# Two decoder layers on one core: the output product of the first cross attention in three fp32r terms, with its operands split by GpSimd

## What is computed

```
q = rmsnorm((x_norm @ Wq + bq) as 16 heads of 128) * qn_w
k = rmsnorm((ctx @ Wk + bk) as 4 heads of 128) * kn_w
v = (ctx @ Wv + bv) as 4 heads of 128           # each serves 4 query heads
probs = softmax(q @ k.T / sqrt(128) + mask)      # 256 x 64 for each head
x = x + tanh(gate) * (concat(probs @ v) @ Wo)
```

## Time and profile before

| what | value |
|---|---|
| median of 3 runs | 1886.22 us (1883.31 to 1887.39) |
| the profiled execution | 1881.76 us, span 1880.0 us |
| mean granted TensorE clock | 0.974 |
| TensorE matmul / weight load busy | 1743.0 us (93%) / 1570.9 us (84%) |
| VectorE, ScalarE, GpSimd busy | 1095.1 (58%), 1318.6 (70%), 1065.5 us (57%) |
| output products of the stage (L765) | 256 passes, from 111.5 to 367.8 us |

### The profile page before, as it was taken

The page is one execution under the profiler, slowest core; times in us unless marked ns, Lnnn a source line. Parts: engine busy times, 40 slices in busy tenths (PEclk is TensorE's granted clock), DMA queues, the critical chain, the costliest instruction groups (busy, mean ns, idle before and its releaser), DMA issues.

```text
span 1880.0 us, 36601 instructions
## 1 busy us (share of the span) xinstructions
PE 1743.0 (93%) x11648; PEld 1570.9 (84%) x11648; DVE 1095.1 (58%) x3073; ACT 1318.6 (70%) x4254; POOL 1065.5 (57%) x1215
## 2 busy tenths in 40 slices
PE   3499999799999999999989996999999999999798
PEld 1388888688999999999978885888888888888797
DVE  1467777757776666566765553555555555565222
ACT  1177777588888878888865444888888888888221
POOL 1433334689999889889832113445454444554454
PEclk9599999899999999999999998999999999999899
DMA  3000001210000000000002100000000000000000
GB/s 115 23 15 18 16 17 41 66 31 13 13 24 18 13 24 13 18 18 12 18 1 79 28 19 8 12 8 12 12 9 12 9 12 13 19 15 12 4 24 23
DMA packets 29392, 40.17 MB, mean 21 GB/s; under 512 B 4882, under 2 KB 18450, under 8 KB 29076
## 3 DMA queue, kind: packets, MB, share of 16 engines
q1 hardware_dynamic: 29204, 37.83, 6.8%
HBM read 33.63 MB, written 4.19 MB: 20 GB/s over the span
## 4 chain that ended last, share of the span: by engine, by line
PE 67%; ACT 13%; issue 5%; POOL 5%; DVE 3%; DMA 0%; POOLq 0%; SPq 0%; ACTq 0%; DVEq 0%
PE pS L1072 4%; PE pF L574 4%; ACT pA L1736 4%; PE pF L576 4%; PE pF L575 4%; PE pA L576 3%; PE pA L574 3%; PE pA L575 3%; PE pA L1063 3%; PE pA L1065 3%; PE pA L1064 3%; PE pS L744 3%; PE pF L765 3%; PE pO L1091 3%; ACT x_P L1762 2%
## 5 line engine op out<-in xcount | busy, mean ns | idle before, releaser
L574 PE MATMUL pA<-Wh,XTh 128*128 128x512 f32 (+1 forms) x512 | 222.0, 434 | 5.7 <-DVEq L117 2.9
L1482 POOL TENSOR_TENSOR f_sw<-f_sw,f_sin 128x512 f32<-128x512 f32 x128 | 181.6, 1419 | 40.8 <-ACT f_sw L1191 40.8
L576 PE MATMUL pA<-Wh,XTl 128*128 128x512 f32 (+1 forms) x512 | 189.1, 369 | 0.0
L575 PE MATMUL pA<-Wl,XTh 128*128 128x512 f32 (+1 forms) x512 | 188.0, 367 | 0.0
L1191 ACT ACTIVATE f_sw<-pA 64x512 f32<-64x512 f32 x256 | 151.5, 592 | 36.0 <-PE pA L1065 32.2
L1485 POOL TENSOR_TENSOR f_sw<-f_sw,f_RB 128x512 f32<-128x512 f32 x128 | 168.8, 1318 | 10.0
L1063 PE MATMUL pA<-XTh,Wh 128*128 128x256 f32 x512 | 163.1, 318 | 8.2 <-DMA wg<-in_w_gate 7.5
L1762 ACT ACTIVATE x_P<-x_P,x_nm 128x192 f32<-128x192 f32 (+1 forms) x256 | 127.5, 502 | 35.8 <-DVE x_nm L1878 35.8
L569 POOL TENSOR_TENSOR Wl<-RAW,Wh 128x256 fp32r<-128x256 f32 (+3 forms) x64 | 60.7, 948 | 155.3 <-ACT Wh L562 155.3
L1065 PE MATMUL pA<-XTh,Wl 128*128 128x256 f32 x512 | 145.3, 284 | 0.0
L1064 PE MATMUL pA<-XTl,Wh 128*128 128x256 f32 x512 | 145.2, 284 | 0.0
(11 more groups left out here) (295 smaller groups left out, 6084.4 us busy)
## 6 DMA issues: line engine op xcount, KB each, us to landing
RAW<-in_w_f SPq DMA_DIRECT2D x32, 256.0 KB, 2.6
RAW<-in_w_x SPq DMA_DIRECT2D x32, 160.0 KB, 2.2
RAW<-in_w_x SPq DMA_DIRECT2D x32, 128.0 KB, 2.0
RAW<-in_w_ff SPq DMA_DIRECT2D x8, 288.0 KB, 2.8
R<-in_x SPq DMA_DIRECT2D x4, 512.0 KB, 6.0
x_spill<-R SPq DMA_DIRECT2D x8, 256.0 KB, 2.0
RAW<-in_w_moe SPq DMA_DIRECT2D x8, 256.0 KB, 2.7
moe_xs<-x_spill SPq DMA_DIRECT2D x8, 256.0 KB, 3.1
```

What stands on the lines that cost most here:

```text
L574: e.matmul(o, ah, bh, start=first, stop=False)
L575: e.matmul(o, ah, bl, start=False, stop=False)
L576: return e.matmul(o, al, bh, start=False, stop=last)
L1482: e.tensor_tensor(y, y, bc(sind[:, :], 1, 2), ALU.mult).then_inc(q["swm"], 1)
```

## The change

GpSimd gets two new steps. `split_vw(j)`, once per pair in the even body, splits VW into VWh and VWl, 1024 columns each. `split_p(i)`, once per iteration and one body later, splits PT into PTh and PTl, 512 columns each. Each is a cast and a subtraction. `out_proj` takes the four split tensors and makes three fp32r products out of each float32 one, 12 instead of 8 passes, and waits for the subtractions (`pl`, `vwl`) instead of ScalarE's copies. VW has one buffer instead of two; so `vw_ev` waits for the `split_vw` before it. The copy to PT waits for `pl` in place of `f`.

```diff
-            VW = sb("x0_VW", [P, 2, 2, 2, D], F32, x0)
+            VW = sb("x0_VW", [P, 2, 2, D], F32, x0)
+            VWh = sb("x0_VWh", [P, 2, 2, 2, D], F32R, x0)
+            VWl = sb("x0_VWl", [P, 2, 2, 2, D], F32R, x0)
+            PTh = sb("x0_PTh", [P, 2, 2, S], F32R, x0)
+            PTl = sb("x0_PTl", [P, 2, 2, S], F32R, x0)
...
+                def split_vw(j):
+                    e.wait_ge(q["vwe"], 2 * j + 2)
+                    e.wait_ge(q["f"], pos(2 * j - 2))
+                    e.tensor_copy(VWh[:, j % 2], VW[:, :, :, :]).then_inc(q["vwh"], 1)
+                    e.wait_ge(q["vwh"], j + 1)
+                    e.tensor_tensor(VWl[:, j % 2], VW[:, :, :, :], VWh[:, j % 2].bitcast(F32), ALU.subtract
+                                    ).then_inc(q["vwl"], 1)
+
+                def split_p(i):
+                    e.wait_ge(q["pte"], i + 1)
+                    e.wait_ge(q["f"], pos(i - 1))
+                    e.tensor_copy(PTh[:, i % 2], PT[:, i % 2]).then_inc(q["ph"], 1)
+                    e.wait_ge(q["ph"], i + 1)
+                    e.tensor_tensor(PTl[:, i % 2], PT[:, i % 2], PTh[:, i % 2].bitcast(F32), ALU.subtract
+                                    ).then_inc(q["pl"], 1)
...
                         low_w(e, q["hi"], q["split"], CW_X0, i, s, (i // 8 + 1) % 2)
+                    if i:
+                        split_p(i - 1)
+                    if s == 0:
+                        split_vw(i // 2)
                     if s == 1 and not last:
                         vs(i + 1)
...
                 in_order(e, NI, body, 24)
+                split_p(NI - 1)
...
                 def out_proj(i, s):
-                    e.wait_ge(q["pte"], i + 1)
-                    e.wait_ge(q["vwe"], pos((i - s if not isinstance(i, int) else 2 * (i // 2)) + 2))
+                    e.wait_ge(q["pl"], i + 1)
+                    e.wait_ge(q["vwl"], i // 2 + 1)
                     e.wait_ge(q["acc"], i)
                     for t in range(T):
                         for hp in range(2):
-                            ins = e.matmul(pF[:, t * D:(t + 1) * D], PT[:, s, hp, t * P:(t + 1) * P],
-                                           VW[:, i // 2 % 2, s, hp, :], start=(hp == 0), stop=(hp == 1))
+                            r = slice(t * P, (t + 1) * P)
+                            ins = three(e, pF[:, t * D:(t + 1) * D], PTh[:, s, hp, r], PTl[:, s, hp, r],
+                                        VWh[:, i // 2 % 2, s, hp, :], VWl[:, i // 2 % 2, s, hp, :],
+                                        hp == 0, hp == 1)
...
                 def vw_ev(i, hp):
                     e.wait_ge(q["vw"], i + hp + 1)
-                    e.wait_ge(q["f"], pos(i - 2))
+                    e.wait_ge(q["vwl"], i // 2)
...
-                    e.wait_ge(q["f"], pos(i - 1))
+                    e.wait_ge(q["pl"], pos(i - 1))
                     e.activation(PT[:, s, :, :], pS[:, 1, :].rearrange("p (a n) -> p a n", a=2), ACT.Copy
                                  ).then_inc(q["pte"], 1)
```

More of the change, by code:

```diff
@@ L641, in cross_attention_0 @@
                      "sc", "s1", "s2", "mx", "s3", "ex", "sm", "rs", "pn", "pt", "pte", "f", "acc",
-                     "vhi", "vs", "vw", "vwe")
+                     "vhi", "vs", "vw", "vwe", "vwh", "vwl", "ph", "pl")
             q = {x: sem("x0_" + x) for x in names}
@@ L830, in vw_ev @@
                     e.wait_ge(q["vw"], i + hp + 1)
-                    e.wait_ge(q["f"], pos(i - 2))
+                    e.wait_ge(q["vwl"], i // 2)
                     for r in range(2):
                         for par in range(2):
-                            ins = e.activation(VW[par * SC:(par + 1) * SC, i // 2 % 2, r, hp, :],
+                            ins = e.activation(VW[par * SC:(par + 1) * SC, r, hp, :],
                                                pO[r * SC:(r + 1) * SC, par * D:(par + 1) * D], ACT.Copy)
```

## The result

The changed kernel takes 1940.35 us (median of 4; before 1886.39), a ratio of 1.0289 with a 95% interval of 1.0271 to 1.0306: 54 us slower. The forecast was 1934 us, range 1911 to 1956.

What follows compares the result with a forecast made beforehand. TensorE was taken to bound the kernel. Start 2.5, steady 21.4 plus 0.6 for the wider low_w(25), and tail 23 gave +47.5 on 1881.8, 1929.3; the median stands 4.5 above, so 1934 us, range 1911 to 1956.

Steps and rivals of the forecast that it cites:

- Products: TensorE's output product: twelve fp32r passes save 0.22 us per iteration, 0.44 per pair, if TensorE stays the bound.
- One sign: Steady part: pairs 18 to 18.8 us; GpSimd releases odd bodies' first output product, or VectorE the transposes.
- The pair: Two iterations of the first cross attention's steady part: 18.4 us, 1.94 more than before.
- VectorE's route: Softmax: L902 waits 2.3 us for split_vw's subtraction; exp, query copies, scores follow, putting the output product at 18.5.
- the queue's route: Loop through GpSimd's queue, split_vw, norms, low_w, split_p, then the output product: 17.1 us per pair.
- two orders of L902 and the subtraction: In the softmax, either L902 waits 2.3 us or the subtraction waits 0.65; both orders give a pair of 18.4.
- the rival that I kept out of the sum: TensorE idle time brings 1.2 GHz: 1.6 us more in each of 12 pairs, 1953 us; chance 0.14.
- The tail: out_proj(24) to out_proj(31): GpSimd, never out of work, is the bound; 23 us more.
- The start: Bodies 0 to 2, with split_vw(0) and split_p(0) ahead of the first output product: 2.5 us more.
- the holding up: VectorE and GpSimd delay each other when both read SBUF at length; raises the pair from 17.1 to 18.4.
- the rival without it: Long reads do not meet: pair 17.1, start 1.5, steady 7, tail 21, +29.5, 1916 us; chance 0.15.
- The lock: VectorE and GpSimd reading SBUF: the second waits for nearly the whole first; norms would add 1 us per pair, left out.

Runs made afterwards that it cites:

- run without long reads: Changed kernel with GpSimd's splits replaced by operations of the same length that read 8 columns, high parts standing in for low ones: 1924.75 us, ratio 1.0209.
- run with the idle time filled: Changed kernel plus two unused float32 products of 512 columns on TensorE ahead of the scores in odd bodies 3 to 25: 1930.78 us, ratio 1.0241.
- splits unused: Changed kernel with the splits kept but the earlier float32 output product, waiting for ScalarE's copies alone, and two VW buffers again: 1943.4 us, ratio 1.0306.
- halves: Changed kernel with split_vw done in two halves of 512 columns, each waiting for ScalarE's copy of that half alone: 1922.4 us, ratio 1.0194.

## Why the prediction was right

**The bound and where the splits stand.** Right: TensorE was the bound, GpSimd had the time, and it was what the long work meets that cost. Products: 0.22 us per iteration predicted, (16.46 - 15.9) / 2 = 0.28 found. One sign was wrong: in the steady part TensorE waits ahead of the scores, for ScalarE's copy of the queries, and not for GpSimd ahead of the product or for VectorE ahead of the transposes.

**Prices.** Casts 0.66 and 1.18 predicted, 0.61 and 1.04 us found when left alone; subtractions 1.28 and 2.40, found 1.27 and 2.40 at the least. The casts cost 1.2 ns per column at 512 and 1.0 at 1024. The Trainium skill ("GPSIMD Engine Reference", "Reconciling with measured numbers") puts the best case at 1.8 cycles per element, which is an estimate of 1.5 ns at the 1.2 GHz that it works with; by this trace the casts are faster.

**The pair.** 18.4 predicted, 19.02 measured. By the runs 1.70 of the 2.56 us over before are VectorE's route (18.16); it alone would set the pair, and the queue's route (17.35, 0.89 over before) lies under it. The other 0.86 is the clock. Of my two orders of L902 and the subtraction, the trace shows the first: the mask additions come second and wait, and the route over the scores, which I put at 18.5, is the one that ends last. The forecast without the clock was 0.24 us too long per pair. The step that was mis-sized is the rival that I kept out of the sum: the clock. I took it as an all-or-nothing case at 1.6 us per pair; it is there in about every second pair and worth 0.86 in the mean. With it the pairs run from 18.3 to 19.7, not from 18 to 18.8 as my sign had it.

**The tail.** 23 predicted, 22.6 measured; without the splits there, 23.8 us of it come back, 26 with the pair ahead of it. The count of GpSimd's work was right because it is the bound there, and a bound's time is a plain sum.

**The start.** 2.5 predicted, without its working; 5.9 measured. Before `out_proj(0)` the chain of the odd body is the same: exp waits 3.3 us, because the mask additions take 3.15 us in place of 0.76, and the scores that follow run at 1.2 GHz (3.67 us). Of the 2.5 the holding up was 1.0 (the rival without it has 1.5), and the clock had no term.

**The sum.** The range held with room, but the nearness of 1934 to 1940 is in part luck. In the profiled executions +47.5 stands against +58.0: the steady part was 6.1 short (28.1 against 21.4 + 0.6), the start 3.4, the stretch behind the stage 1.4, and the tail 0.4 too long. Of these 10.5 us the medians hide 4, since the profiled execution of before was a quick one. The 1.4 us behind the stage can't be told from the spread: in the nine other runs, whose later stages are the same, this stretch takes 1514.9 to 1520.6 us.

**The lock.** The Trainium skill ("SBUF — State Buffer", "Who interferes with whom") has VectorE instructions with two SBUF inputs wait for a GpSimd instruction that reads SBUF. For the long splits the trace agrees (2.76 us against 0.76). For the small power over 8 columns it doesn't: in the run without long reads GpSimd was about as busy, and the mask additions took 0.44 us in the mean.

**The clock.** In the odd body above, TensorE was idle for 2.0 us and then got 1.2 GHz. The Trainium skill ("TensorE: Matmul & The Clock Gate", "A second HAM failure mode: psum-queue depth-cycling") describes for another kernel a clock that falls and rises in turn from short idle times between groups of matmuls; the run with the idle time filled agrees.

## What to carry to other kernels

- An engine with 10 of 16 us free can still make the period longer: lay the new work into its queue and follow what waits behind it, with the period as the unknown. Then do the same for the engine that its long reads hold up, since they move that engine's chain. In the steady part cutting the read in two took 1.5 us off each pair, where taking 4.1 us of work per pair from GpSimd took 0.2.
- Where two routes are nearly equally long, removing the longer leaves the other (18.16 and 17.35 us here), and shortening the shorter shows little. Test each alone, and ask which wait ends last.
- A new idle time on TensorE can cost twice: itself, and the lower clock behind it. How often isn't told by its length alone: over eleven pairs the clock fell six times with 1.9 us per pair (changed kernel), eight times with 1.6 (splits unused), once with 1.0 or 1.4 (halves, no long reads).

## What was not expected

Unused work made the kernel faster: 1.88 us of float32 products per pair took 0.86 us off each pair, because TensorE stayed at 2.4 GHz. In the changed kernel the clock fell in about every second pair, behind an idle time of about 2.0 us before the scores; no run here tells why in some pairs and not in others.
